# Weight loads in four half-size slots, and the layer-norm sums moved behind their matmul loops

## What is computed

```
x = inputs                                     # (4, 2048, 4096)
# layer 0a: local attention, with blocks of 128 tokens
y = conv1d(x, conv_w, kernel 3, SAME) + conv_b  # 4096 -> 3*1024
q, k, v = split(y)                              # 1024 each
q, k, v = q @ wq + bq, k @ wk + bk, v @ wv + bv # 16 heads of 64
p = softmax(causal(q k^T / 8))                  # within blocks of 128
o = (p v) @ wo + bo                             # 1024 -> 1024
x = layernorm(x + o @ proj_w + proj_b)          # 1024 -> 4096
# layer 0b
x = layernorm(x + x @ W.T + b + ((x @ A) * probs) @ B)   # 4096 -> 4096, rank 256 beside it
```

## Time and profile before

| | |
|---|---|
| median of 3 runs | 2469.77 us (2466.6 to 2473.04) |
| the profiled execution, its own time | 2473.42 us |
| its span on the slowest core (core 0) | 2471.6 us |
| spans of all cores | 2452.4 to 2471.6 us |
| TensorE busy (PE) | 1901.2 us, 77% of the span |
| ScalarE busy (ACT) | 301.9 us, 12% |
| VectorE busy (DVE) | 231.5 us, 9% |
| GpSimd busy (POOL) | 391.3 us, 16% |
| mean granted TensorE clock, core 0 | 0.925 |

### The profile page before, as it was taken

One profiled execution on the slowest core, in us unless ns is written; L12 is line 12 of the kernel. 1 busy time (PEld: TensorE's weight loads), 2 busy tenths in 40 slices (PEclk: granted clock), 3 DMA queues, 4 the chain that ended last, 5 costly groups with the idle time before them and its releaser, 6 DMA issues.

```text
span 2471.6 us, 20030 instructions; the slowest of 8 cores (2452.4 to 2471.6 us)
## 1 busy us (share of the span) xinstructions
PE 1901.2 (77%) x8591; PEld 835.1 (34%) x8762; DVE 231.5 (9%) x158; ACT 301.9 (12%) x413; POOL 391.3 (16%) x344
## 2 busy tenths in 40 slices
PE   0499999999999999999555575562788888888800
PEld 0144444444444444444222122221333333333300
DVE  0000000000000000001421021006000000000078
ACT  0000000000000000012254152220011111111110
POOL 1112121212121212100001101116000000000068
PEclk9999999999999999999668798896899999999955
DMA  9969898999989898920215746545425435254024
GB/s 149 93 64 86 80 85 81 84 83 81 86 79 87 73 81 72 81 30 6 34 23 75 96 55 87 78 65 70 66 34 69 54 49 68 35 68 56 13 112 160
DMA packets 415819, 176.11 MB, mean 71 GB/s; under 512 B 301555, under 2 KB 399987, under 8 KB 415476
## 3 DMA queue, kind: packets, MB, share of 16 engines
q0 software_dynamic: 404928, 157.32, 58.9%
q1 hardware_dynamic: 10804, 17.50, 2.0%
HBM read 315.32 MB, written 16.78 MB: 134 GB/s over the span
## 4 chain that ended last, share of the span: by engine, by line
PE 71%; DMA 8%; ACT 6%; issue 6%; POOL 5%; DVE 3%; another core or an unknown queue 1%; ACTq 0%; POOLq 0%; DVEq 0%
PE psA L335 20%; PE psB L335 20%; PE psA L1047 17%; DMA xjb<-xT 6%; PE psA L794 3%; POOL ob L1112 2%; POOL ob L1108 2%; ACT sqtmp L1005 2%; PE psA L685 1%; PE psA L392 1%; PE psB L392 1%; PE psA L1057 1%; PE psA L930 1%; PE psB L1023 1%
## 5 line engine op out<-in xcount | busy, mean ns | idle before, releaser
L335 PE MATMUL psA<-xb,cwb 128*128 128x512 bf16 x2258 | 498.3, 379 | 100.6 <-DMA cwb<-cw 98.1
L335 PE MATMUL psB<-xb,cwb 128*128 128x512 bf16 x2258 | 496.7, 378 | 2.6
L335 PEld LDWEIGHTS psA<-xb,cwb 128*128 128x128 bf16 x2304 | 223.3, 97 | 374.3 <-issue 101.0
L335 PEld LDWEIGHTS psB<-xb,cwb 128*128 128x128 bf16 x2304 | 222.9, 97 | 275.7 <-issue 1.5
L298 POOL DMA_DIRECT2D cwb<-cw x144 | 164.8, 1174 | 842.5 <-PE psA L335 415.1
L1047 PE MATMUL psA<-x1bA,wsF 128*128 128x512 bf16 x999 | 227.5, 382 | 16.7 <-DMA Bmb<-Bm 13.7
L1047 PEld LDWEIGHTS psA<-x1bA,wsF 128*128 128x128 bf16 x1024 | 100.5, 98 | 132.7 <-issue 17.9
L1047 PE MATMUL psA<-x1bB_lo,wsF 128*128 128x512 bf16 x504 | 114.9, 379 | 2.1 <-ACT sqtmp L1005 1.7
L1047 PE MATMUL psA<-x1bB_hi,wsF 128*128 128x512 bf16 x505 | 115.2, 379 | 0.4
L959 POOL DMA_DIRECT2D wsF<-Wt x16 | 26.8, 1678 | 556.5 <-PE psB L1023 442.1
L1023 PE MATMUL psB<-sqtmp,ones_s 128*128 128x512 bf16 x62 | 24.0, 386 | 88.5 <-ACT sqtmp L1005 88.4
(11 more groups left out here) (161 smaller groups left out, 1176.7 us busy)
## 6 DMA issues: line engine op xcount, KB each, us to landing
cwb<-cw POOLq DMA_DIRECT2D x144, 512.0 KB, 22.6
wsF<-Wt POOLq DMA_DIRECT2D x16, 2048.0 KB, 15.6
outT<-ob SPq DMA_DIRECT2D x64, 256.0 KB, 2.2
xb<-xT POOLq DMA_DIRECT2D x4, 2052.0 KB, 44.4
wsA<-projw POOLq DMA_DIRECT2D x8, 1024.0 KB, 9.6
wsB<-projw POOLq DMA_DIRECT2D x8, 1024.0 KB, 10.3
xjb<-xT POOLq DMA_DIRECT2D x64, 128.0 KB, 4.9
wqpre<-wq POOLq DMA_DIRECT2D x8, 256.0 KB, 34.7
```

What stands on the lines that cost most here:

```text
L335: return e.matmul(pbank(bank), buf[:, (w * 32 + dc) * 128:(w * 32 + dc + 1) * 128], xb[:, dc * (T + 2) + tokc * 512 + w: dc * (T + 2) + to ...
```

## The change

Three things are changed.

1. The weights of `wo` and of the projection come in column groups of 256 (512 KB for each load). Each of `wsA` and `wsB` is cut in two, which gives four slots with a semaphore each; group g goes to slot g % 4 and serves two tiles. Both halves of `emit_p4` use this.
2. The second half's layer norm sums are no longer interleaved with the projection (`emit_ln1_stat` isn't called any more). Both halves now use the loop behind the projection (L842, L851, L859), with banks 0 and 1. `emit_ht` uses banks 2 and 3 always, so that it doesn't touch these.
3. In the feed-forward loop `emit_stats2` isn't called between the tiles. All 64 calls stand behind the loop, first the 32 of half 0, then the 32 of half 1. `emit_stats2` itself is as it was.

```diff
-    SEMS = ("xS", "c0", "c1", "w2", "s0", "s1", "sD", "gC",
+    SEMS = ("xS", "c0", "c1", "w2", "s0", "s1", "s2", "s3", "sD", "gC",
...
+        def _wslot(g):
+            t = wsA if g % 2 == 0 else wsB
+            half_off = 2048 * ((g // 2) % 2)
+            return (t[:, half_off:half_off + 2048],
+                    ("s0", "s1", "s2", "s3")[g % 4])
...
-        emit_wo_load(0)
-        emit_wo_load(1)
+        for g in range(4):
+            emit_wo_load(g)
...
-            if wc % 4 == 3:
-                stream_free[par] = ("tC", t_grp)
+            if wc % 2 == 1:
+                slot_free[g % 4] = ("tC", t_grp)
...
         def emit_pw_load(g):
-            par = g % 2
-            buf = wsA if par == 0 else wsB
-            sem = "s0" if par == 0 else "s1"
+            buf, sem = _wslot(g)
             waits = []
-            if stream_free[par] is not None:
-                waits.append(stream_free[par])
+            if g % 4 in slot_free:
+                waits.append(slot_free[g % 4])
             def pwdma(e, g=g, buf=buf):
-                src = projw[:, g * 512:(g + 1) * 512].rearrange(
+                src = projw[:, g * 256:(g + 1) * 256].rearrange(
                     "(c p) f -> p c f", p=128)
...
-        emit_pw_load(0)
-        emit_pw_load(1)
+        for g in range(4):
+            emit_pw_load(g)
         emit_xj_load(0)
         emit_xj_load(1)
...
-            if dmc % 4 == 3 and dmc // 4 + 2 < 8:
-                emit_pw_load(dmc // 4 + 2)
+            if dmc % 2 == 1 and dmc // 2 + 4 < 16:
+                emit_pw_load(dmc // 2 + 4)
             if dmc + 2 < DC:
                 emit_xj_load(dmc + 2)
-            if half == 1:
-                pend_stats.append(dmc)
-                if len(pend_stats) > 4:
-                    emit_ln1_stat(pend_stats.pop(0))
-        if half == 1:
-            while pend_stats:
-                emit_ln1_stat(pend_stats.pop(0))
-            st["b1"], st["b2"], st["t_stats"] = 4, 5, S.n("tC")
-            st["res1_evac"] = res1_evac
-            ln_state[half] = st
-            return
-        b1, b2 = (0, 1) if half == 0 else (4, 5)
+        b1, b2 = 0, 1
...
     def emit_ht(half):
         for erc in range(ERC):
-            bank = p45_bank(tile_i)
+            bank = 2 + erc
...
                 res2_writes[(oc, half)] = c_evac
                 tile_i += 1
-                pend_stats2.append((oc, half, c_evac))
-                if len(pend_stats2) > 4:
-                    emit_stats2(*pend_stats2.pop(0))
         stream_free[par] = ("tC", S.n("tC"))
         if pg + 2 < 16:
             emit_wt_load(pg + 2)
-    while pend_stats2:
-        emit_stats2(*pend_stats2.pop(0))
+    for half in range(2):
+        for oc in range(DC):
+            emit_stats2(oc, half, res2_writes[(oc, half)])
```

More of the change, by code:

```diff
@@ L636, in build_nc @@
     stream_free = {0: None, 1: None}
+    slot_free = {}
     ln_state = {}
@@ L650, in hit_slot @@
             slot_i[0] += 1
+        def _wslot(g):
[3 more added lines that the diff above has]
+                    ("s0", "s1", "s2", "s3")[g % 4])
         wo_ld = {}
         def emit_wo_load(g):
-            par = g % 2
-            buf = wsA if par == 0 else wsB
-            sem = "s0" if par == 0 else "s1"
+            buf, sem = _wslot(g)
             waits = [("tC", p2_t_end)]
-            if stream_free[par] is not None:
-                waits.append(stream_free[par])
+            if g % 4 in slot_free:
+                waits.append(slot_free[g % 4])
             def wodma(e, g=g, buf=buf):
-                src = wo[:, g * 512:(g + 1) * 512].rearrange(
+                src = wo[:, g * 256:(g + 1) * 256].rearrange(
                     "(c p) f -> p c f", p=128)
-                dst = buf[:, :].rearrange("p (c f) -> p c f", c=8)
+                dst = buf.rearrange("p (c f) -> p c f", c=8)
                 return e.dma_start(out=dst, in_=src)
@@ L674, in emit_p4 @@
             hit_slot()
-            g = wc // 4
-            par = g % 2
-            buf = wsA if par == 0 else wsB
+            g = wc // 2
+            buf, _ = _wslot(g)
             bank = tile_i % 4
@@ L686, in womm @@
                         pbank(bank),
-                        buf[:, hec * 512 + (wc % 4) * 128:
-                            hec * 512 + (wc % 4) * 128 + 128],
+                        buf[:, hec * 256 + (wc % 2) * 128:
+                            hec * 256 + (wc % 2) * 128 + 128],
                         otb[:, hec * 1024 + hofs:hec * 1024 + hofs + 512],
@@ L782, in emit_p4 @@
             hit_slot()
-            g = dmc // 4
-            par = g % 2
-            buf = wsA if par == 0 else wsB
+            g = dmc // 2
+            buf, _ = _wslot(g)
             xcb = xjb0 if dmc % 2 == 0 else xjb1
@@ L795, in pmm @@
                         pbank(bank),
-                        buf[:, wc * 512 + (dmc % 4) * 128:
-                            wc * 512 + (dmc % 4) * 128 + 128],
+                        buf[:, wc * 256 + (dmc % 2) * 128:
+                            wc * 256 + (dmc % 2) * 128 + 128],
                         a1b[:, wc * TH:(wc + 1) * TH],
@@ L807, in emit_p4 @@
             xj_free[dmc % 2] = ("tC", t_grp)
-            if dmc % 4 == 3:
-                stream_free[par] = ("tC", t_grp)
+            if dmc % 2 == 1:
+                slot_free[g % 4] = ("tC", t_grp)
+            if dmc == DC - 1:
+                stream_free[0] = stream_free[1] = ("tC", t_grp)
             pw_ = [("tC", t_grp)]
```

## The result

The changed kernel takes 2420.0 us (median of 10 executions), the kernel before 2469.2 us beside it: a ratio of 0.9795, with a 95% interval of 0.9784 to 0.9805, so 49 us less. The forecast was 47.5 us less.

A forecast was written before the change was run, and what follows sets the result against it. The prediction took late operations, not full engines, as the bound: TensorE waiting for ACT's square and for x. Its terms, +0.9 - 30.5 + 12.4 - 30.3 = -47.5 us, gave 2425.9, stated as 2422 us; range 2385 to 2458.

The forecast's parts named there:

- The stall in the feed-forward loop: Between feed-forward tiles, a sum waits for ACT's square behind an evacuation; without it, tiles fall from 9.64 to 7.55 us.
- The chain: Behind the feed-forward loop, 64 steps of square and sum through one slot, 1.55 us each at 1.2 GHz.
- Part 3's term: Feed-forward loop and the sums moved behind it: -30.3 us together; -46 at 1.30 us a step, -11 at 1.85.
- The 1.85 us bound: Sums behind the feed-forward loop: each step as long as the old trace's last one, 2441 us in all; chance 0.16.
- Part 2's loop: Behind the second half's projection: sums take 24.8 us, then `emit_ht(0)` without waiting for weights; +12.4 us.
- The second half's projection: Two tiles take 8.2 us with half-size loads, against 10.37 behind a 1024 KB load; -30.5 us, sums' stalls included.
- the twelve periods: Second half's projection: twelve pairs of tiles with a 512 KB load ahead of x, 8.2 us each, 98.4 us.
- the three undisturbed pairs: End of the second half's projection: three pairs without a weight load between, 6.1 us each, 18.3 us.
- The first half's projection: Two waits of 9.5 us for four tiles replace one of 12.1 us and three quick tiles; +0.9 us.
- A saving of only 1.2 us for halving a load: Projection loads' landing mostly fixed: pairs of 9.2 and 10.9 us, 2454 us in all; chance 0.10.
- the loads shrink to 7.5 us a pair: Projection, both halves: -25 and -39 us instead of +0.9 and -30.5, 2388 us in all; chance 0.12.
- the stall in the feed-forward loop stay: Another wait stands behind it, weights or a bank; tiles lose only two sum matmuls, 2525 us in all; chance 0.02.

The follow-up runs named there:

- lag: Changed kernel with feed-forward squares between the tiles again and TensorE's two sum matmuls behind the next tile's matmuls: 2374.0 us, ratio 0.9580.
- chain2: Changed kernel with two slots used in turn for the squares behind the feed-forward loop: 2372.2 us, ratio 0.9594.
- part 1 alone: Kernel before with four half-size weight slots, layer norm and feed-forward sums still between the tiles: 2459.5 us, ratio 0.9942.
- part 2 alone: Kernel before with the second half's sums in a loop of their own, loads still 1024 KB: 2458.5 us, ratio 0.9935.

## Why the prediction was right, step by step

- **The stall in the feed-forward loop.** Right in place and cause. Evacuations are 7.55 us apart (475.9 us for 63, forecast 475.7), the weights keep up (they land in 19.1 us now and 15.6 before, and have 30.2), and the clock is 1.00. `lag` shows the cause: with the same squares between the tiles, moving two matmuls one tile later in TensorE's list removes the stall.
- **The chain.** Forecast 1.55 us a step, at 1.2 GHz; measured 1.51 at that clock, and 1.49 over the 63 steps, because the first ones ran at 1.30. Part 3's term was -30.3 us and measured -33.5. The 1.85 us bound, taken from the last step of the trace before, did not come up again; why that one step was longer was not tried. `chain2` shows that the wait of each square for the sum before it, through the single slot, set the pace.
- **Part 2's loop.** Forecast +12.4 us, measured +12.4 on the way to the loop. `emit_ht(0)` waits for nothing (in the changed kernel its 64 matmuls run from 1633.06 without a gap), so the load was covered as said.
- **The second half's projection.** Forecast -30.5 us, measured -26.9 with the gap ahead of it. The size was near, but the prediction put the term under part 1, with the remark that it includes the sums' stalls. The runs put it under part 2: alone, with loads as they were, it gives -25.1 of the -25.4 us that the projection itself lost. The two parts don't add: part 1 alone gives -12.0 there, and with part 2 made only -1.9. The prediction's own model would have said so, had it been applied to 1024 KB loads without sums: 10.4 us for the pair behind a load and 6.1 for the other is 16.5 us for four tiles, against twice 8.2. Halving the load did save what was forecast, 10.6 to 8.5 us for a pair behind a load (part 2 alone and the changed kernel, means of the six cores whose records are complete), but it made twice as many such pairs. There is luck in how near the sum came: the twelve periods took 8.5 us on average and not 8.2, the three undisturbed pairs 4.9 and not 6.1, and the two errors cancel.
- **The first half's projection.** Forecast +0.9, measured -0.8 at its end, made of a start 3.4 us earlier and a course 2.6 us longer. So the pair period was right in kind: one long wait became two shorter ones of about the same sum. Its size was not: 9.5 us were forecast, and the pairs without attention take 8.3. The 12.13 us it came from was core 0's; the mean over the eight cores is 10.9, and core 0 had the longest first half before (132.8 us against a mean of 125.6). The saving of 2.6 us was right, and the excess stood in the time before as well, so the difference hardly saw it.
- **The rivals.** A saving of only 1.2 us for halving a load did not hold, neither as a time (2454 us) nor in the pairs, which would be 9.2 us long. That part 1 gave nothing in company of part 2 has another reason, the number of such pairs. Neither did the loads shrink to 7.5 us a pair, nor did the stall in the feed-forward loop stay. The Trainium skill ("DMA: Bandwidth & Descriptors", section "Anatomy of one DMA") gives each load a fixed part of 2.0 us; here the weight loads' median landing went from 9.6 us (`wsA`, in the page of the kernel before) to 6.4 us at half the size, more than its formula's 1.2 us, so the measurement doesn't agree with its size.

So the sum was right, and the parts were near; one of them was booked under the wrong edit, and two sizes in it were off and cancelled. The gain is that of parts 2 and 3.

## What to carry to other kernels

When an engine waits for a short helper operation of another engine, look at what that helper stands behind in its own list, and move the consumer one iteration later: this gave 67 us more than moving all of it behind the loop, where the same work became a ping-pong at half the clock (with two slots instead of one that ping-pong alone gives back 48 of the 67). A stall that lies in a stage where a load is late as well is worth only what the load leaves of it: 25 of 40 us turned into a wait for x. Before loads are cut or reordered, find whether they are late or the bytes are too many; reordering two issues gave 23 us in the two stages and 10 to 18 in the kernel's time, and issuing them four tiles ahead ran into the rate.

## What the runs showed of the hardware that was not expected

- Once the loads were issued four tiles ahead, on all 8 cores, the DMA engines were at a share of 1.05 and brought 112 GB/s, though a stretch inside a single load had 207 GB/s at 1.24. Half the bytes per weight load gave 4.8 instead of 6.3 us for a pair of tiles. With 1024 KB loads the share was only 0.88 (mean of the cores in the second half), but the rate was 110 GB/s, much as at 0.99 with 512 KB: the share alone does not tell how near the limit is. What takes the rate away was not tried.
- In the chain TensorE was shown busy for 61 of 91 us, in matmuls between waits; the clock fell to the 1.2 GHz level behind the fourth sum of squares (2213.30) and stayed there to the chain's end. With the squares in two slots TensorE was busy 20.3 of 25 us, and the clock was 1.00. So two slots gave 0.58 us a step by ACT's pace (1.30 to 0.72 us) and 0.21 us by the clock (1.51 to 1.30).
